# Decoder layer on one core: copies, fill order, last normalisation and PE filler matmuls in attention's last iterations

## The chip, the cores and the metric
The kernel runs on one core of a Trainium2 chip. The metric is the device time of one execution in microseconds (us). A core has five engines that run beside each other and meet at semaphores: PE (TensorE, matrix products and transposes), DVE (VectorE), ACT (ScalarE), POOL (GpSimd) and SP, which here issues DMAs. Each engine takes its instructions in the order in which they were written.

## The reference
The input `x` is 16 blocks of 128 rows by 256 columns. Three sublayers follow each other, each closed by a residual sum and a layer norm over the row.

1. Differential self-attention with 16 heads: `qkv = x @ w_qkv.T`, a rotary turn of q and k, two softmax products whose difference is taken (`sdpa(q1, k1) - lam * sdpa(q2, k2)`), a group norm, and `@ wo.T`.
2. Cross attention over a given context `ctx_512` (16 x 128 x 64): 32 query heads of size 8 share 8 key/value heads; keys and values are both the context.
3. A mixture of experts: a router gives sigmoid scores, the two best of 8 experts are used with normalised weights, and two shared experts see every row. Each expert is `(silu(x @ wg.T) * (x @ wu.T)) @ wd.T`.

Every product must be close to float32. The kernel reaches this by splitting an operand into a float16 high part and a float16 low part (`hi` and `lo`) and adding three products.

## The kernel before
The kernel has two parts: an attention part (both attentions and the router, `build`) and an experts part (`experts`). The second starts when all engines have left the first.

The attention part is a software pipeline over the 16 blocks b. Each engine has a function `body(n)` that is called for n = 0 to 22. In iteration n, stage k works on block n - k where `live(n - k)` holds (0 to 15). Names that begin with `a_` or use `A` belong to self-attention, `c_` or `C` to cross attention. The stages that matter here:

- n - 3, cross attention's stacking. PE transposes the stacked keys (`stack_k`, L905 at the bottom of `stack_T`) and queries (`stack_q`) of the block into one PSUM bank, `c_one`. ACT copies each out of it: `kt_in` (L502, into `c_kt`) and `qm_in` (L494, into `c_qm`). Both use the same bank, so `stack_q` waits for the copy of the keys; and `kt_in` waits until PE has read the previous block's keys for the last time (the eighth `exp_scores` of block n - 4).
- n - 3, at its end, and n - 4. PE fills eight banks of scores (`max_scores`, L937), two of them in iteration n as `max_scores(C, n - 3, 0)` and `1`, six at the beginning of the next. DVE takes the largest of each (`largest`, L680). There are two banks, so fill f waits for the reduction of fill f - 2.
- n - 4. When all eight maxima are there, PE transposes the queries again with their maxima (`restack`, L905), DVE copies them (`reqt_in`, L674), and PE fills eight banks of scores for the exponentials (`exp_scores`, L954), which ACT computes (`exp`, L514), again with two banks. `values_cross` (L982) multiplies the first four with the values (product 0), then the other four (product 1). ACT copies the results out (`ot_in`, L520), and PE turns them back (`back_T`, L992).
- n - 5. DVE divides (`cross_divide`, L749) and scales (`cross_mix`, L756), POOL adds the residual (`cross_add`, L393), DVE takes mean and variance (L706 and L766).
- n - 6. POOL computes the reciprocal root (`power`, L378 and L380) and normalises the block (`normalise`, L385). PE transposes it (`x2_T`, L1023), ACT and DVE split it (`x2_high` L531, `x2_low` L771).
- n - 7. PE computes the router's logits (`route`, L879), DVE copies them out (`logits`, L777).

The order of the work is the order in each engine's `body`. PSUM banks are shared in a fixed cycle (`RINGS` and `Turns`): a PE step waits for the reader of the bank's last content. From n = 16 on self-attention's stages run dry, from n = 19 on cross attention's too. The last blocks then go through with little else beside them.

`keep_warm(k)` (L1037) is k float16 products of 128x128 weights with 240 columns whose result nobody reads. Before the change it is used only for n = 0 to 3, into the bank of `c_one`.

The experts part begins on PE with `group_T(0)` (L1675, eight float32 transposes). ACT and DVE split their result, and PE begins the first expert step (`split_products`, L1684).

Of the kernel before, what the change touches and what calls it, by code (L numbers as in the profile page):

```python
# [15 lines left out]
ALU = mybir.AluOpType  # L16
# [3 lines left out]
P = 128  # L20
B, S, E = 16, 128, 256
# [40 lines left out]
ITERATIONS = B + 7  # L62
WARM = 240
SHARED_HIGH = 3


class Steps:
# [41 lines left out]
def build(nc, a, out):  # L109
    ctx = ExitStack()  # L110
    sems = ExitStack()
    with sems, ctx:
# [116 lines left out]
        def live(b):  # L229

            return 0 <= b < B
# [52 lines left out]
        def _(pool):  # L284
# [110 lines left out]
            def body(n):  # L395

                if live(n - 3):
                    group_norm(n - 3)
                if live(n - 1):
                    q_low(n - 1)  # L400
                if live(n - 4):
                    cross_v(n - 4)
                if live(n - 1):
                    k_low(n - 1)
                if live(n - 6):
                    power(C.mv, C, n - 6, C.s_mv)
                if live(n - 3):
                    cross_k_low(n - 3)
                if live(n - 6):
                    normalise(C.y, C.mv, C, n - 6, x2_ready)  # L410
                if live(n - 5):
                    cross_add(n - 5)
                if live(n - 3):
                    power(A.mv2, A, n - 3, A.s_mv2)
                    normalise(A.y2, A.mv2, A, n - 3, x1_ready)
                if live(n - 2):
                    mix_sub(n - 2)
                if live(n - 3):
                    cross_q_low(n - 3)
                if live(n - 2):  # L420
                    group_scale(n - 2)
                if live(n):
                    rope_sum(n)
# [6 lines left out]
        def _(act):  # L430
# [103 lines left out]
            def body(n):  # L534

                if live(n - 5):
                    ot_in(C, n - 5, 1)
                if live(n - 2):
                    exp(A, n - 2, 0)
                    exp(A, n - 2, 1)  # L540
                if live(n - 1):
                    q_high(n - 1)
                    k_high(n - 1)
                if live(n - 2):
                    exp(A, n - 2, 2)
                    exp(A, n - 2, 3)
                if live(n - 3):
                    y_high(n - 3)
                if live(n - 2):
                    exp(A, n - 2, 4)  # L550
                    exp(A, n - 2, 5)
                    exp(A, n - 2, 6)
                if live(n - 1):
                    kt_in(A, a_one, n - 1)
                if live(n - 2):
                    exp(A, n - 2, 7)
                if live(n - 3):
                    cross_k_high(n - 3)
                if live(n - 2):
                    ot_in(A, n - 2, 0)  # L560
                    ot_in(A, n - 2, 1)
                if live(n - 4):
                    exp(C, n - 4, 0)
                    exp(C, n - 4, 1)
                if live(n - 1):
                    v_in(n - 1)
                if live(n - 4):
                    exp(C, n - 4, 2)
                    exp(C, n - 4, 3)
                if live(n - 6):  # L570
                    x2_high(n - 6)
                if live(n):
                    x_high(n)
                if live(n - 4):
                    exp(C, n - 4, 4)
                    exp(C, n - 4, 5)
                if live(n - 3):
                    cross_q_high(n - 3)
                    kt_in(C, c_one, n - 3)
                if live(n - 4):  # L580
                    exp(C, n - 4, 6)
                    exp(C, n - 4, 7)
                if live(n - 3):
                    qm_in(C, c_one, n - 3)
                if live(n - 4):
                    ot_in(C, n - 4, 0)
                k, half = divmod(n - SHARED_HIGH, 2)
                if 0 <= k < NSH * 3:
                    split_high(act, 0, k, wsh[:, k // 3, k % 3, 0, :], half)
                if live(n - 1):  # L590
                    reqt_in(A, a_one, n - 1)
# [8 lines left out]
        def _(dve):  # L600
# [107 lines left out]
            def moments(t, bn, mv, b, s_bn, s_mv):  # L708

                dve.wait_ge(s_bn, b + 1)  # L710
                dve.memset(t.pad[:], 0.0)
                dve.bn_aggr(mv[:], bn[:]).then_inc(s_mv, 1)
# [47 lines left out]
            def cross_moments(b):  # L760
# [4 lines left out]
                dve.memset(C.pad[:], 0.0)  # L765
                dve.bn_aggr(C.mv[:], C.bn[:]).then_inc(C.s_mv, 1)  # L766

            def x2_low(b):

                dve.wait_ge(A.s_x2hi, b + 1)  # L770
                dve.tensor_tensor(A.x2t_lo[:], c_one[:, 0:E].rearrange("p (c n) -> p c n", c=EC), A.x2t_hi[:],  # L771
                                  ALU.subtract).then_inc(A.s_x2lo, 1)
# [6 lines left out]
            def body(n):  # L779
# [38 lines left out]
                if live(n - 2):  # L818
                    mix_half(n - 2, 1)
                    mix_half(n - 2, 0)  # L820
                if live(n - 6):
                    x2_low(n - 6)
                if live(n - 1):
# [6 lines left out]
                    largest(A, n - 1, 6)  # L830
                if live(n - 2):
                    moments(A, A.bn, A.mv, n - 2, A.s_bn, A.s_mv)
                if live(n - 1):
                    largest(A, n - 1, 7)
                if live(n - 2):
# [10 lines left out]
                    rope_first(n)  # L846
                if live(n - 5):
                    cross_moments(n - 5)
                if live(n):
                    rope_straight(n)  # L850

# [10 lines left out]
        def _(pe):  # L862
# [171 lines left out]

            warm_in = id32[:].bitcast(F16)

            def keep_warm(k):  # L1037

                for _ in range(k):
                    pe.matmul(ps[:, 5, 512 - WARM:], warm_in[:, 0:P], warm_in[:, 0:WARM], start=True, stop=True)  # L1040

            def body(n):

# [49 lines left out]
                    restack(C, c_one, n - 4)  # L1093
                if live(n - 3):
                    out_project(n - 3)
                if n == 1:
                    keep_warm(8)
                if live(n - 1):
# [7 lines left out]
                if live(n - 4):  # L1106
                    exp_scores(C, n - 4, 0)
                    exp_scores(C, n - 4, 1)
                if live(n - 1):
                    max_scores(A, n - 1, 2)  # L1110
                    max_scores(A, n - 1, 3)
                    if n == 1:
                        keep_warm(4)
                    project_v(n - 1)
# [8 lines left out]
                    exp_scores(C, n - 4, 3)  # L1123
                if live(n - 1):
                    max_scores(A, n - 1, 5)
                if live(n - 6):
                    x2_T(n - 6)
                if live(n):
                    x_T(n)
                if n == 0:  # L1130
# [15 lines left out]
                    project_qk(n)  # L1146
                if n == 0:
                    keep_warm(36)
                if live(n - 3):
                    stack_q(C, c_one, n - 3)  # L1150
                if live(n - 2):
                    group_mean(n - 2)
                if 1 <= n < 3:
                    keep_warm(8)
                if live(n - 4):
# [2 lines left out]
                    restack(A, a_one, n - 1)  # L1158
                if 1 <= n < 3:
                    keep_warm(16)  # L1160
                if live(n - 3):
                    max_scores(C, n - 3, 0)
                    max_scores(C, n - 3, 1)
                if live(n - 4):
# [714 lines left out]
```

## Time and profile before

| what | value |
|---|---|
| median of 3 runs | 847.19 us (843.85 to 848.7) |
| profiled execution: device time | 847.25 us |
| profiled execution: span from first to last instruction | 845.0 us |
| mean granted TensorE clock | 0.961 |
| PE busy | 773.2 us (92%) |
| DVE, ACT, POOL busy | 521.2, 519.8, 308.9 us |
| attention part | 0 to 430.1 us of the span |
| experts part | 430.1 to 845.0 us |

Times in the trace are microseconds from the start of the span. "Granted clock" is the share of full speed that the chip gives PE: 1.00 is 2.4 GHz and 0.50 is 1.2 GHz. In a row of a timeline the first number is the start, the second the duration, and what stands in square brackets at its end is how long the engine had been idle before and who ended that.

### The profile page before, as it was taken

To read this page: it belongs to the slowest core of one execution; us is meant where nothing else is said; L and a number is where in the kernel's file an instruction comes from. 1 tells how busy PE (TensorE), PEld (TensorE's weight loads), DVE (VectorE), ACT (ScalarE), POOL (GpSimd) and SP (SyncE) were. 2 spreads that over 40 slices of the span, in tenths; PEclk is the share of its full clock that TensorE was granted. 3 is DMA by queue.
4 is the path that set the end of the run, shared out by engine and by line. 5 is a ranking of instruction groups with operands and counts; after the bars stand their busy time and mean duration, and the time that the engine had idled before them with its cause. 6 is when DMAs were issued, how large, how long until landed. Compare 5 with 4: busy or idle time off the path is not lost.

```text
span 845.0 us, 19993 instructions
## 1 busy us (share of the span) xinstructions
PE 773.2 (92%) x7621; PEld 508.9 (60%) x7621; DVE 521.2 (62%) x1188; ACT 519.8 (62%) x948; POOL 308.9 (37%) x481
## 2 busy tenths in 40 slices
PE   6888999999999999997869899999999999999993
PEld 5555555555555555554435455557878888787652
DVE  3346788888888888865338866764444444444353
ACT  2445788888888888775425554545555655555353
POOL 3134455555555555544210573001222222222222
PEclk9998999999999999998569999999999999999998
DMA  8800000000010100000033676422332322223231
GB/s 247 246 2 1 2 2 33 3 24 11 2 33 2 33 2 2 2 2 1 1 97 97 194 233 201 150 89 51 47 50 45 52 45 49 48 45 52 54 104 63
DMA packets 38282, 51.02 MB, mean 60 GB/s; under 512 B 9264, under 2 KB 33072, under 8 KB 38192
## 3 DMA queue, kind: packets, MB, share of 16 engines
q1 hardware_dynamic: 31040, 40.39, 16.1%
q0 software_dynamic: 7152, 9.34, 6.6%
q8 instruction: 66, 1.08, 0.6%
q14 instruction: 24, 0.20, 0.1%
HBM read 31.04 MB, written 18.68 MB: 59 GB/s over the span
## 4 chain that ended last, share of the span: by engine, by line
PE 39%; DVE 5%; DMA 3%; ACT 2%; issue 1%; POOL 0%; ACTq 0%; POOLq 0%; DVEq 0%
PE ps L1684 34%; PE ps L1763 3%; DMA wst<-in_wx 3%; DVE wr L224 1%; PE ps L1743 1%; DVE ht_lo L1561 1%; DVE th L1556 1%; ACT wr L215 1%; PE ps L1675 0%; ACT th L1402 0%; DVE xg_lo L1549 0%; ACT ht_hi L1407 0%; POOL e_rs L1376 0%; PE ps L1709 0%; ACT xg_hi L1394 0%
## 5 line engine op out<-in xcount | busy, mean ns | idle before, releaser
L1363 POOL DMA_INDIRECT acc<-y_sb,xin x39 | 60.5, 1552 | 220.0 <-ACT y_sb L1431 220.0
L1684 PE MATMUL ps<-wr,xr_hi 128*128 x624 | 129.3, 299 | 0.0
L1402 ACT ACTIVATE th<-ps 128x384 f32<-128x384 f32 (+1 forms) x118 | 57.9, 491 | 108.6 <-PE ps L1684 103.6
L1684 PE MATMUL ps<-xg_hi,wsh 128*128 128x512 f16 x320 | 103.2, 385 | 4.8 <-DVE xg_lo L1549 4.8
L680 DVE TENSOR_REDUCE c_qs<-ps 128x4 f16<-128x512 f32 x128 | 84.0, 693 | 22.6 <-PE ps L937 21.0
L680 DVE TENSOR_REDUCE a_qs<-ps 128x4 f16<-128x512 f32 x128 | 85.1, 689 | 19.7 <-PE ps L937 18.7
L1684 PE MATMUL ps<-wr,xr_lo 128*128 x312 | 93.4, 299 | 0.0
L514 ACT ACTIVATE a_pt<-ps 128x512 f32<-128x512 f32 x128 | 74.5, 595 | 30.4 <-PE ps L954 28.5
L1556 DVE SCALAR_TENSOR_TENSOR th<-th,ps 128x384 f32<-128x384 f32 (+1 forms) x118 | 65.2, 553 | 34.5 <-ACT th L1402 34.4
L514 ACT ACTIVATE c_pt<-ps 128x512 f32<-128x512 f32 x128 | 69.8, 604 | 19.3 <-PE ps L954 19.1
L1643 DVE COPY ht<-ps 128x512 f16<-128x512 f16 x39 | 16.5, 424 | 93.7 <-PE ps L1763 93.7
L1684 PE MATMUL ps<-wr,ht 128*128 x585 | 70.4, 273 | 0.7 <-issue 0.7
L1684 PEld LDWEIGHTS ps<-wr,xr_hi 128*128 128x128 f16 x624 | 59.4, 98 | 18.2
L1684 PEld LDWEIGHTS ps<-wr,ht 128*128 128x128 f16 x585 | 57.0, 98 | 8.0 <-issue 1.3
L1684 PE MATMUL ps<-xg_lo,wsh 128*128 128x512 f16 x160 | 61.6, 385 | 0.0
L1684 PE MATMUL ps<-wsh,ht_hi 128*128 128x256 f16 x320 | 54.7, 273 | 5.4 <-DVE ht_lo L1561 5.2
L1561 DVE TENSOR_TENSOR hs<-th,hs 128x384 f16<-128x384 f32 x78 | 38.3, 492 | 29.1 <-ACT hs L1407 29.1
L1407 ACT ACTIVATE hs<-th 128x384 f16<-128x384 f32 x78 | 36.6, 470 | 31.9 <-DVE th L1556 31.9
L1684 PEld LDWEIGHTS ps<-xg_hi,wsh 128*128 128x128 f16 x320 | 31.7, 99 | 40.6 <-issue 6.8
L948 PE MATMUL ps<-mask,id 128*128 128x512 f16 x128 | 50.2, 392 | 3.2 <-ACT a_qt L508 3.1
L954 PE MATMUL ps<-a_qt,a_kt 32*128 32x128 f16 x512 | 51.0, 219 | 0.0
L954 PEld LDWEIGHTS ps<-a_qt,a_kt 32*128 32x128 f16 x512 | 28.7, 93 | 32.8 <-issue 32.8
(211 smaller groups left out, 1751.1 us busy)
## 6 DMA issues: line engine op xcount, KB each, us to landing
wst<-in_wx SPq DMA_DIRECT2D x30, 640.0 KB, 4.6
xs<-zero SPq DMA_DIRECT2D x1, 5031.0 KB, 19.9
xin<-xs SPq DMA_DIRECT2D x39, 129.0 KB, 2.1
acc<-x_row SPq DMA_DIRECT2D x4, 512.0 KB, 3.3
x_row<-acc SPq DMA_DIRECT2D x8, 256.0 KB, 5.2
out<-x_row SPq DMA_DIRECT2D x8, 256.0 KB, 2.1
x_row<-in_x SPq DMA_DIRECT2D x1, 1536.0 KB, 10.8
wst<-in_wqkvT SPq DMA_DIRECT2D x1, 768.0 KB, 4.8
```

Source lines behind the costliest of these rows:

```text
L514: act.activation(t.pt[:, f, :, :].rearrange("p j n -> p (j n)"), score_bank(t, "e", b, f), ACT.Exp, scale=(E // HEADS if t is A else SD) * ...
L680: dve.tensor_reduce(t.qs[:].rearrange("p (c i) s -> p c i s", i=NI)[:, c:c + 4, f % 4, USED], score_bank(t, "m", b, f).rearrange("p (j n) ...
L948: pe.matmul(o.rearrange("p (j n) -> p j n", j=NI), id16[:], mask4[:].unsqueeze(1).to_broadcast([P, NI, P]), start=True, stop=False, skip_g ...
L954: ins = pe.matmul(o[:, j * P:(j + 1) * P], t.kt[r, c, :], t.qt[r, c, :], start=t is C, stop=True, skip_group_check=t is A)
L1363: pool.indirect_dma_start(acc, bass.IndirectOffsetOnAxis(ap=row, axis=0), y_sb[:, n % 2, :], None, compute_op=ALU.add).then_inc(f_acc, 16)
L1402: act.activation(th[:, k % 2, 0:n], gate[:, k % 2, 0:n], ACT.Silu, scale=1.0 / WSCALE).then_inc(f_th, 1)
L1407: act.activation(dst, th[:, k % 2, 0:dst.shape[-1]], ACT.Copy).then_inc(f_hhi, 1)
L1556: dve.scalar_tensor_tensor(out=t, in0=t, scalar=1.0 / WSCALE, in1=up[:, k % 2, 0:n], op0=ALU.mult, op1=ALU.mult).then_inc(f_hid, 1)
L1561: dve.tensor_tensor(dst, th[:, k % 2, 0:dst.shape[-1]], hi, ALU.subtract).then_inc(f_hlo, 1)
L1643: dve.tensor_copy(ht[:, HALVES[1][0]:, :, :].rearrange("p j r n -> p (j r n)"), htp[1]).then_inc(f_hTin[1], 1)
L1684: ins = pe.matmul(o, l[x], r[y], start=(first and n == 0), stop=(last and n == m - 1), skip_group_check=not (first and last))
L1763: ins = pe.transpose(htp[half][:, o:o + P], hs[:, r, j * P:(j + 1) * P], id16[:])
```

## The change
`LAST = B + 1` is 17, the first iteration without a block of self-attention in stage n - 1. The edits act from n = 17 on.

- The two copies `kt_in` and `qm_in` of cross attention go from ACT to DVE for n = 17 and 18 (blocks 14 and 15). On DVE `kt_in` stands behind `x2_low(n - 6)`, ahead of the moments of block n - 5, and `qm_in` behind these.
- For n = 17 and 18 PE's `max_scores(C, n - 3, 0)` and `1` stand ahead of `values_cross(n - 4, 1)`, no longer behind it.
- `normalise` of block 15 goes from POOL to DVE (`last_normalise`), in n = 21.
- `keep_warm` gets a bank as argument and is called in n = 17 to 21 with `a_one`, a bank that no stage uses by then: 8 products ahead of `stack_q` (n = 17, 18); 6 behind the place of `out_project` and 4 behind the second `exp_scores` (n = 18, 19); 10 ahead of product 1 (n = 19); 8 ahead of `x2_T` (n = 20, 21) and 5 behind it (n = 19, 20, 21). By iteration, n = 17 to 21, that is 8, 18, 25, 13 and 13 products.

```diff
@@ POOL body
-                if live(n - 6):
+                if live(n - 6) and n - 6 < B - 1:
                     normalise(C.y, C.mv, C, n - 6, x2_ready)
@@ ACT body
                     cross_q_high(n - 3)
-                    kt_in(C, c_one, n - 3)
+                    if n < LAST:
+                        kt_in(C, c_one, n - 3)
...
-                if live(n - 3):
+                if live(n - 3) and n < LAST:
                     qm_in(C, c_one, n - 3)
@@ DVE
+            def last_normalise():
+
+                dve.wait_ge(C.s_rstd_ok, B)
+                dve.tensor_scalar(x_all[:, B - 1, :], C.y[:], C.mv[:, 0:1], C.rstd[:, 0:1], ALU.subtract, ALU.mult
+                                  ).then_inc(x2_ready, 1)
@@ DVE body
+                if n - 6 == B - 1:
+                    last_normalise()
                 if live(n - 6):
                     x2_low(n - 6)
...
                     moments(A, A.bn, A.mv, n - 2, A.s_bn, A.s_mv)
+                if live(n - 3) and n >= LAST:
+                    kt_in(C, c_one, n - 3)
...
                 if live(n - 5):
                     cross_moments(n - 5)
+                if live(n - 3) and n >= LAST:
+                    qm_in(C, c_one, n - 3)
@@ PE
-            def keep_warm(k):
+            def keep_warm(k, bank=c_one):
 
                 for _ in range(k):
-                    pe.matmul(ps[:, 5, 512 - WARM:], warm_in[:, 0:P], warm_in[:, 0:WARM], start=True, stop=True)
+                    pe.matmul(bank[:, 512 - WARM:], warm_in[:, 0:P], warm_in[:, 0:WARM], start=True, stop=True)
@@ PE body
                     out_project(n - 3)
+                if n in (LAST + 1, LAST + 2):
+                    keep_warm(6, a_one)
...
                     exp_scores(C, n - 4, 1)
+                if n in (LAST + 1, LAST + 2):
+                    keep_warm(4, a_one)
...
+                if n in (LAST + 3, LAST + 4):
+                    keep_warm(8, a_one)
                 if live(n - 6):
                     x2_T(n - 6)
+                if n in (LAST + 2, LAST + 3, LAST + 4):
+                    keep_warm(5, a_one)
...
+                if n in (LAST, LAST + 1):
+                    keep_warm(8, a_one)
                 if live(n - 3):
                     stack_q(C, c_one, n - 3)
+                if n == LAST + 2:
+                    keep_warm(10, a_one)
                 if live(n - 2):
                     group_mean(n - 2)
+                if n >= LAST and live(n - 3):
+                    max_scores(C, n - 3, 0)
+                    max_scores(C, n - 3, 1)
...
                 if live(n - 4):
                     values_cross(n - 4, 1)
...
-                if live(n - 3):
+                if live(n - 3) and n < LAST:
                     max_scores(C, n - 3, 0)
                     max_scores(C, n - 3, 1)
```

## Rows read from the trace of the kernel before

**Rows 1.** The page's 40 slices of 21.1 us: granted TensorE clock in tenths.
```profile
PEclk9998999999999999998569999999999999999998
```

**Rows 2.** Busy time by stage of the drain; columns: stretch, length, busy us (instructions) per engine, clock, DMA.
```profile
366.70:386.04 19.34, 17.56 (x214) 9.98 (x211) 11.43 (x32) 15.50 (x29) 8.54 (x17) 1.00 0.00 1
386.13:404.56 18.43, 15.19 (x129) 8.19 (x130) 8.81 (x22) 9.06 (x18) 7.87 (x17) 0.72 0.00 1
404.56:422.98 18.42, 14.98 (x111) 8.29 (x112) 7.68 (x18) 6.09 (x12) 4.55 (x7) 0.58 0.00 1
422.98:430.10 7.12, 1.73 (x17) 0.81 (x15) 2.48 (x10) 0.77 (x2) 2.61 (x5) 0.50 0.00 0
430.10:439.33 9.23, 7.69 (x24) 3.71 (x25) 1.53 (x3) 3.28 (x5) 0.32 (x2) 0.55 0.65 192
```

**Rows 3.** The same view, in stretches between changes of the granted clock.
```profile
387.14:390.56 3.42, 2.70 (x32) 1.65 (x30) 3.34 (x7) 0.99 (x3) 1.73 (x6) 1.00 0.00 0
390.56:393.97 3.41, 3.16 (x20) 2.07 (x21) 2.49 (x7) 0.00 (x0) 2.51 (x3) 0.50 0.02 5
393.97:397.38 3.41, 2.64 (x31) 1.46 (x34) 1.55 (x6) 3.00 (x7) 1.95 (x3) 1.00 0.00 0
...
400.80:404.21 3.41, 2.92 (x20) 1.09 (x22) 0.00 (x0) 2.84 (x5) 0.00 (x0) 0.50 0.00 0
404.21:407.62 3.41, 2.69 (x34) 1.67 (x32) 3.06 (x6) 0.60 (x1) 2.16 (x4) 1.00 0.02 5
```

**Rows 4.** Groups by line, 366.6 to 430.1 us: busy, mean ns, idle before.
```profile
L680 DVE TENSOR_REDUCE c_qs<-ps 128x4 f16<-128x512 f32 x24 | 15.2, 690 | 11.2 <-PE ps L937 10.9
L514 ACT ACTIVATE c_pt<-ps 128x512 f32<-128x512 f32 x24 | 13.0, 600 | 13.3 <-PE ps L954 13.3
...
L385 POOL TENSOR_SCALAR x_row<-c_y,c_mv,c_rstd 128x256 f32<-128x256 f32 x5 | 6.1, 1225 | 0.3
...
L674 DVE COPY c_qt<-ps 128x1024 f16<-128x1024 f16 x3 | 2.1, 691 | 1.3 <-PE ps L905 1.2
...
L502 ACT ACTIVATE c_kt<-ps 128x1024 f16<-128x1024 f16 x2 | 2.0, 1023 | 2.5 <-PE ps L954 2.5
```

**Rows 5.** PE's timeline, 383 to 428 us.
```profile
383.58 0.61 PE L905 MATMUL ps<-id,c_qs 128*128 128x128 f16 x8 [1.31 <-ACT c_kt L502]
...
384.71 1.07 PE L982 MATMUL ps<-c_pt,c_v 128*32 128x512 f32 x8 [0.34 <-DVE a_g L730]
...
393.95 0.41 PE L954 MATMUL ps<-c_qt,c_kt 32*128 32x128 f16 x8
...
401.29 1.01 PE L905 MATMUL ps<-id,c_qs 128*128 128x128 f16 x8 [1.31 <-ACT c_kt L502]
402.24 1.93 PE L982 MATMUL ps<-c_pt,c_v 128*32 128x512 f32 x8
...
411.66 0.61 PE L954 MATMUL ps<-c_qt,c_kt 32*128 32x128 f16 x8 [0.79 <-DVE c_qt L674]
...
418.90 1.94 PE L982 MATMUL ps<-c_pt,c_v 128*32 128x512 f32 x8 [1.16 <-ACT c_pt L514]
...
422.77 0.63 PE L1023 MATMUL ps<-id,x_row 128*128 128x128 f32 x2
...
427.58 0.69 PE L1023 MATMUL ps<-id,x_row 128*128 128x128 f32 x2 [2.85 <-POOL x_row L385]
```

**Rows 6.** DVE's timeline, 423 to 425 us.
```profile
423.86 0.42 DVE L771 TENSOR_TENSOR a_x2t_lo<-ps,a_x2t_hi 128x256 f16<-128x256 f32 x1
424.65 0.43 DVE L706 BATCH_NORM_STATS2 c_bn<-c_y 128x6 f32<-128x256 f32 x1 [0.37 <-POOL c_y L393]
```

**Rows 7.** PE's timeline at the kernel's beginning: `keep_warm`.
```profile
3.59 5.11 PE L1040 MATMUL ps<-id 128*128 128x240 f16 x26
...
28.38 1.80 PE L1040 MATMUL ps<-id 128*128 128x240 f16 x16
```

**Rows 8.** The chain that ended last, behind the attention part: start, us, what.
```profile
433.58 5.10 PE ps L1684 x12
```

More of the change, by code:

```diff
@@ L64 @@
 SHARED_HIGH = 3
+LAST = B + 1
 class Steps:
```

## Prediction
> **What bounds the kernel now.** I read the page's slices first. The granted clock is near full except at the kernel's edges and in three slices about 380 to 443 us [rows 1], where attention runs dry. The stage table comes next: the last full iteration of the drain has clock 1.00, the two after it 0.72 and 0.58, the tail of the last block 0.50, the entry into the experts 0.55 [rows 2]. No engine is saturated there: in 404.56 to 422.98 PE is busy 14.98 of 18.42 us, DVE 7.68, ACT 6.09, and each works while the others wait. It is one block's chain: eight reductions on DVE, a transpose and a copy, eight exponentials on ACT, two value products, two transposes and copies for the next block, then again. The bounds of the stages are the starts of DVE's reductions of blocks 14 and 15, 386.13 and 404.56; 422.98 is the end of block 15's last transpose back. So each iteration's length is the chain's length, and PE's speed enters it wherever PE is the one awaited: the stack transposes take 0.61 at full clock and 1.01 at half, the value product 1.07 and 1.93 [rows 5].
>
> What the clock does: in 387.14 to 390.56 PE only hands small score fills to DVE (busy 2.70 of 3.42, though), and the clock falls to half at its end. In 390.56 to 393.97 it has transposes and the output projection with hardly a gap, and the clock returns. In 393.97 to 397.38 it waits for ACT between fills (2.64), and it falls. In 400.80 to 404.21 a stack and a value product stand back to back, and it returns. In the fills for DVE after that (2.69) it falls again [rows 3] and stays at half to the end of attention and 8 us beyond: 0.58, 0.50, 0.55 [rows 2].
>
> The Trainium skill (TensorE: Matmul & The Clock Gate, "Why this matters for your kernels") asks for no long idle gaps between bursts. By that rule alone the clock would not have fallen here, because PE is busy four fifths of each of those stretches; the trace disagrees. By the rule the filler products would change no clock and be pure cost, which is rival C below; by the rows they stand where gaps preceded a fall.
>
> **The change part by part.** The sum is made against the profiled execution, 847.25 us, which lies at the median, 847.19.
>
> *Price of a filler product.* 16 took 1.80 at full clock, so 0.10 each after a tail of about 0.2; 26 took 5.11 near the start, 0.19 to 0.20 each, which is twice that and so the price at half [rows 7].
>
> *n = 17 (clock 1.00).* The key copy goes from 1.02 on ACT to 0.69, the price of DVE's copy of the same shape [rows 4], and the query copy likewise: 0.33 each. The 8 fillers (0.8) lie in the 1.31 us in which PE awaits the key copy [rows 5], 0.95 after the change, so they cost 0. DVE then starts block 14's reductions about 0.7 early. But value product 1 (0.85 of issue) and a transpose back (0.45) now stand behind the first two score fills and ahead of the third, for which DVE waits after two reductions (1.3 us). Before, the product lay under the query copy. So nearly all is given back: 0.15 gained (bounds 0 and 0.7).
>
> *n = 18.* The reductions (15.2 busy for 24, so 0.64 each [rows 4]) are as before, and so is the fall of the clock. Behind the output projection PE went straight into the exponentials' fills at 393.95, with no idle time [rows 5]: 6 fillers there are on the chain, 0.6 at full clock and 1.2 at half; the clock returned at 393.97, so 0.5 lost (bounds 0.4 and 1.2). The 4 fillers behind the second fill lie in a wait for ACT, at 0. They fill the stretch whose gaps came before the fall, so I take full clock up to the next reductions. What that gives, each term a half-clock duration less a full-clock one: product 0 about 0.5, key stack 0.4, two fills 0.2, query stack 1.01 - 0.61 = 0.4 [rows 5]; the two copies 0.33 each [rows 4]; product 1, which ended at 404.17, some 0.8 behind the query copy (401.29 + 1.01 + 1.03 = 403.4), leaves the chain, 0.75. Together 2.9, less 0.5, against 0.3 of finer overlaps: DVE starts 2.7 early. Product 1 and the transpose ahead of the third fill take 0.5 back. Gained 2.2 (bounds 0.3, if the clock stays at half and 8 fillers of 1.6 outlast the wait, and 3.2).
>
> *n = 19.* The reductions let the clock fall again. At half, the transposed queries and 6 fillers (1.2) end 0.3 behind DVE's copy, so the first fill is 0.3 late. The fillers, the transposes and the fills stand close together, as in 390.56 to 393.97, so I expect the return 1 to 2 us into the exponentials; 4 fillers partly at half cost 0.4 to 0.5 once. At full clock this leg is ACT's: 24 exponentials are 13.0 busy, 0.54 each [rows 4]; 0.43 to the first, four (2.2), `x2_high` 0.4, two (1.1), 0.4 behind product 0, two (1.1): product 1 begins 5.6 behind the first fill. It was 418.90 - 411.66 = 7.24 [rows 5], so 1.65. The 10 fillers (1.0) lie in the wait for the last exponential, 1.16 before. Product 1 gives 1.94 - 1.07 = 0.87. Its end to 422.98 was 2.14 and becomes about 1.35 (copy 0.6, four transposes at full clock 0.6): 0.8. Sum 3.3, less 0.8: 2.5 (bounds -2.6, worked out under C, and 3.5).
>
> *n = 20 and 21.* The 8 fillers ahead of block 14's `x2_T` push it back by 0.8. DVE's `x2_low(14)` stands ahead of the statistics of block 15, and started 0.79 before them [rows 6]; behind the fillers it ends some 0.3 after POOL's sum is ready: 0.3 lost (1.5 at half clock). The last normalisation was 1.22 on POOL [rows 4]. DVE has no such row, so bounds: 0.17, a tiny operation, and 0.69; I take 0.42, that of the 128x256 operations [rows 6]. 0.8 gained. The last `x2_T` at full clock: 0.2. The other fillers lie under POOL's power and under ACT's and DVE's split. Sum 0.7.
>
> The Trainium skill (VectorE: DVE Perf Modes, the errata section's cycle table) gives an SBUF-source operation 58 cycles plus elements over the mode's factor at 0.96 GHz, an estimate of 0.2 us for this one; by it the sum would gain another 0.2. No row here shows this operation in SBUF.
>
> *Entry into the experts.* The mean clock of 0.55 over 430.10 to 439.33 [rows 2] says that half clock held until about 438.3. Eight transposes and 12 products (5.10) are on the chain there [rows 8], 7 us of PE at half; all at full clock would save 3.4. But PE waits about 1.5 between them for the split (9.23 less 7.69 busy) and has little before; I expect the clock to hold for a part, 1.4 (bounds 0 and 3.4). DVE's routing work follows PE's first result, so this passes on.
>
> Sum: 0.15 + 2.2 + 2.5 + 0.7 + 1.4 = 7.0. 847.25 - 7.0 = **840.2 us**.
>
> **The rivals.** B, the clock comes back in one of the two long iterations only, or returns late in each: where the changes of clock fall against the work decides that, and the runs of before differ by 4.9 us among themselves. That loses some 2 of the drain's 5.6 and the entry's 1.4: gain 3.5, **843.7**.
>
> C, the fillers pay for nothing (slower): the clock doesn't return, and they cost 0.2 each wherever PE is awaited. n = 18: 1.2 ahead of the fills, 0.3 beyond the wait ahead of the query stack, less 0.33 and 0.7 of copy and reorder, +0.5. n = 19: 0.3, 0.4, 1.0 (5 ahead of fill 4) and 0.9 (10 at 2.0 in 1.16), +2.6. n = 20: +1.5. Normalisation -0.8. Sum +3.8: **851.0**. It decides once n = 19's fillers run at half. For it: PE was already busy four fifths and lost its clock. Against: each return followed dense work, and fillers are the densest there is.
>
> D, the clock also holds through reductions and entry: 2 more at the entry, 1 at n = 19: **837**.
>
> E, the drain gains its 5.6, but the entry gives nothing, since PE waits there with the clock gone or the constants' loads come last: **841.7**.
>
> F, the change doesn't do what it says: the score fills put ahead gain DVE nothing, as the third comes no earlier. That is in my sum; were it absent, DVE's earlier start would stay, 1.0 more.
>
> **How the numbers follow.** Chances: forecast 0.52 (own range 838 to 843), B 0.22, C 0.09, D 0.07, E 0.10. The range takes D at its low end and B with 3 us of scatter at the high end: 836.5 to 847. Within 0.5% (843.0 to 851.4), about what a measurement can tell from no change, lie three fifths of B, half of C and a little of the forecast: 0.22. Slower, the other half of C and accidents: 0.06. Faster: 0.72.
>
> **What would show it.** Right: granted clock above 0.85 in n = 18 behind the exponentials' start and above 0.8 in n = 19; product 1 of blocks 14 and 15 near 1.07; DVE's reductions of block 15 some 2.7 early, but a gap of about 0.7 behind the second; block 15's chain from its last maximum to its last transpose back 10.7 long, not 13.3; `last_normalise` near 0.42. Wrong: a clock of 0.50 with L1040 at 0.2 each in n = 19; the third fill with no wait; or an experts part longer than the 415 us of before.

## The result, and the profile after

The changed kernel takes 838.87 us (median of 4 runs, 837.29 to 842.1), the kernel before 847.58 (4 runs, 843.85 to 848.7): ratio 0.9915, 95% interval 0.9887 to 0.9944. Run again beside other kernels (e10 below, 5 runs) it took 838.94, ratio 0.9884 (0.9848 to 0.992). The forecast was 840.2. Its total was right. One of its terms was not, and in the profiled execution 2.3 us from outside the changed part made up for it, which is luck.

Line numbers have moved: `max_scores` is L951, `exp_scores` L968, `values_cross` L996, the stack transposes L919, `back_T` L1006, `x2_T` L1037, `keep_warm` L1054, `largest` L682, DVE's copies L671, L664 and L676.

The page's clock line answers to [rows 1]: of the three low slices none below 0.8 is left.

```profile
PEclk9997999999999999999899999999999999999997
```

The stages of the drain, cut at the same events as [rows 2] (first reduction of block 14, of block 15, end of the last transpose back, `group_T`, end of the first silu); columns as there:

```profile
384.81:403.54 18.73, 16.00 (x150) 9.48 (x154) 10.28 (x25) 7.10 (x15) 7.88 (x16) 0.82 0.00 1
403.54:419.92 16.38, 14.87 (x145) 9.08 (x146) 7.79 (x18) 6.30 (x12) 4.86 (x8) 0.90 0.01 2
419.92:426.05 6.13, 3.92 (x42) 2.97 (x40) 2.88 (x11) 0.77 (x2) 1.39 (x4) 1.00 0.00 0
426.05:433.70 7.65, 6.11 (x24) 2.83 (x25) 1.55 (x4) 3.27 (x5) 0.32 (x2) 0.78 0.56 158
```

The second line is 16.38 us long where it was 18.42, the third 6.13 for 7.12. But the first is 18.73 for 18.43: although its clock rose from 0.72 to 0.82, the iteration did not get shorter. The same view in stretches of one clock, against [rows 3]:

```profile
390.98:394.39 3.41, 3.26 (x20) 2.44 (x20) 2.31 (x7) 0.00 (x0) 1.50 (x2) 0.50 0.02 5
394.39:397.80 3.41, 3.15 (x36) 1.78 (x38) 0.57 (x3) 2.86 (x7) 1.98 (x3) 1.00 0.00 0
397.80:401.22 3.42, 3.42 (x28) 1.60 (x21) 0.44 (x2) 1.60 (x5) 0.64 (x1) 0.50 0.00 0
...
408.04:411.46 3.42, 3.42 (x22) 2.58 (x22) 2.81 (x7) 0.00 (x0) 0.73 (x1) 0.50 0.00 0
411.46:428.52 17.06, 13.09 (x135) 8.69 (x133) 4.92 (x19) 8.09 (x17) 3.68 (x8) 1.00 0.03 6
428.52:431.94 3.42, 3.28 (x8) 1.19 (x9) 0.59 (x1) 1.05 (x1) 0.00 (x0) 0.50 0.61 177
```

In n = 18 the clock fell behind 397.80, as it had behind 397.38 before, although the 4 fillers stood ahead and PE was busy for 3.15 of the 3.41 us that led up to it (2.64 before). In n = 19 it came back at 411.46 and stayed to 428.52, through the rest of attention and into the experts; before, it was at half from 407.62 to 438.3. PE's timeline has the steps that [rows 5] has (same columns):

```profile
384.71 1.07 PE L996 MATMUL ps<-c_pt,c_v 128*32 128x512 f32 x8
385.71 0.66 PE L1006 MATMUL ps<-id,c_ot 128*128 128x128 f32 x4
386.30 0.41 PE L951 MATMUL ps<-c_kt,c_qm 24*128 24x128 f16 x8
...
393.22 1.35 PE L1054 MATMUL ps<-id 128*128 128x240 f16 x6
394.51 0.41 PE L968 MATMUL ps<-c_qt,c_kt 32*128 32x128 f16 x8
...
417.41 1.07 PE L996 MATMUL ps<-c_pt,c_v 128*32 128x512 f32 x8
```

The third score fill starts at 386.30, behind the value product and the transpose; that is the reorder's price. The 6 fillers at 393.22 stand between the output projection and the first exponential fill for their full 1.35. Product 1 of block 15 takes 1.07, no longer 1.94. DVE's timeline shows the wait behind the second reduction, and the last normalisation:

```profile
384.81 1.29 DVE L682 TENSOR_REDUCE c_qs<-ps 128x4 f16<-128x512 f32 x2 [0.49 <-PE ps L951]
386.73 2.49 DVE L682 TENSOR_REDUCE c_qs<-ps 128x4 f16<-128x512 f32 x4 [0.63 <-PE ps L951]
...
423.33 0.41 DVE L773 TENSOR_SCALAR x_row<-c_y,c_mv,c_rstd 128x256 f32<-128x256 f32 x1 [0.86 <-POOL c_rstd L381]
```

### The profile page after: what moved, and what is told of

The parts are those of the page before. It is cut to its first block and busy times, and to the rows that moved or that the text cites. A ratio compares the mean times of both kernels' runs of the same rounds, so it can differ in the third digit from the quotient of the medians.

```text
span 837.6 us, 20147 instructions
## 1 busy us (share of the span) xinstructions
PE 774.1 (92%) x7698; PEld 512.9 (61%) x7698; DVE 524.6 (63%) x1193; ACT 516.2 (62%) x944; POOL 309.3 (37%) x480
## 5 line engine op out<-in xcount | busy, mean ns | idle before, releaser
L682 DVE TENSOR_REDUCE a_qs<-ps 128x4 f16<-128x512 f32 x128 | 85.2, 690 | 18.8 <-PE ps L951 17.9
L682 DVE TENSOR_REDUCE c_qs<-ps 128x4 f16<-128x512 f32 x128 | 84.4, 694 | 16.7 <-PE ps L951 15.3
L515 ACT ACTIVATE c_pt<-ps 128x512 f32<-128x512 f32 x128 | 69.7, 603 | 21.1 <-PE ps L968 20.8
L968 PE MATMUL ps<-a_qt,a_kt 32*128 32x128 f16 x512 | 51.8, 222 | 0.0
L968 PEld LDWEIGHTS ps<-a_qt,a_kt 32*128 32x128 f16 x512 | 29.2, 94 | 33.5 <-issue 33.5
```

The lines of the kernel that those rows point to most:

```text
L515: act.activation(t.pt[:, f, :, :].rearrange("p j n -> p (j n)"), score_bank(t, "e", b, f), ACT.Exp, scale=(E // HEADS if t is A else SD) * ...
L682: dve.tensor_reduce(t.qs[:].rearrange("p (c i) s -> p c i s", i=NI)[:, c:c + 4, f % 4, USED], score_bank(t, "m", b, f).rearrange("p (j n) ...
L968: ins = pe.matmul(o[:, j * P:(j + 1) * P], t.kt[r, c, :], t.qt[r, c, :], start=t is C, stop=True, skip_group_check=t is A)
```

## The experiments

The whole difference between two kernels is a few us, and one execution differs from the next by as much. So each kernel's trace was cut at the same events, and the steps are compared as well as the times. t0 is the end of block 13's last exponential fill; "3rd" is the start of the third reduction, "last" the end of the eighth, "fill" the start of the first exponential fill, "back" the end of block 15's last transpose back. One execution each, us:

```
step                  before  changed    e1     e2     e3     e4     e5     e6     e7     e8     e9    e10
t0 to 3rd, b14          5.06     5.09   6.84   5.06   4.74   5.08   5.08   5.46   5.08   4.75   4.75   5.07
3rd to last, b14        4.18     4.19   4.64   4.18   4.18   4.19   5.01   4.20   4.19   5.00   4.59   4.19
last to fill, b14       2.43     3.59   2.48   3.19   3.45   2.47   2.37   3.46   3.39   1.75   1.75   3.33
fill b14 to 1st, b15   10.61     9.03  10.48   8.55   9.26  10.86   7.74   9.83   9.18   7.88   7.89   9.24
1st to 3rd, b15         1.20     1.92   3.46   1.21   1.21   1.93   1.92   1.92   1.92   1.21   1.21   1.92
3rd to last, b15        3.88     3.88   4.08   3.67   3.67   3.69   4.38   3.68   3.89   4.36   4.07   3.88
last to fill, b15       2.02     2.27   2.01   2.36   2.36   2.36   1.61   1.61   2.36   1.61   2.43   2.36
fill to product 1       7.24     5.80   7.26   8.33   5.93   8.35   5.80   5.80   7.88   8.54   5.80   7.83
product 1 to back       4.08     2.51   4.07   2.51   2.51   2.50   2.50   2.50   2.51   2.50   2.51   2.50
back to last route      6.40     5.42   5.53   6.29   5.42   5.42   5.42   5.42   5.42   5.27   5.27   5.43
t0 to group_T          47.86    44.45  51.60  46.10  43.48  47.59  42.58  44.63  46.76  43.81  41.20  46.50
group_T to 1st silu     8.56     6.96   8.76   7.85   7.05   5.36   6.99   6.93   5.36   5.35   5.36   7.80
1st silu to end       406.25   404.52 405.40 407.81 404.87 405.40 404.55 404.81 406.35 405.86 409.84 405.35
```

("Last route" is the start of the fourth of its six products.) Each column is one execution, and some were not typical of their kernel: e1's was the third slowest of 12 (850.23 us, clock 0.948 for a mean of 0.958), e4's the slowest of 12 (845.33, clock 0.967 for 0.973), e10's the slowest of 5.

**e1: everything but the fillers.**

```diff
-                if n in (LAST + 1, LAST + 2):
-                    keep_warm(6, a_one)
...
-                if n == LAST + 2:
-                    keep_warm(10, a_one)
```

> The changed kernel without its 77 filler products; copies, reorder and last normalisation stay. Theory (the clock is what gains): the granted clock stays at about 0.58 in iteration n = 19, product 1 of block 15 takes 1.93, the entry into the experts (start of group_T to the first silu) takes 8.6 us as before, and the kernel gains only 0.33 x 2 from the copies in n = 18, up to 0.7 from the reorder, and 0.8 from the normalisation: 1.5 to 2.3 us, ratio 0.9975. Rival (the engine moves carry it): 5 us or more, ratio 0.994 or lower, at an unchanged clock.

Measured: 845.97 (12 runs, 841.38 to 852.07), ratio 0.9995 (0.9966 to 1.0024). The engine moves alone give nothing that can be measured. The medians are 0.6 apart where 1.5 to 2.3 were expected, and the interval takes in both. In its trace, one of its slow executions, the clock fell once and stayed at half for 58 us:

```profile
384.54:442.56 58.02, 44.67 (x291) 23.14 (x292) 23.24 (x57) 17.18 (x33) 15.19 (x31) 0.50 0.09 27
```

The normalisation's gain is there all the same: back to last route 5.53 for 6.40. At half clock the reorder is worse than at full: the wait behind the second reduction is 2.17, for 0.63 in the changed kernel.

```profile
385.71 1.29 DVE L682 TENSOR_REDUCE c_qs<-ps 128x4 f16<-128x512 f32 x2 [0.70 <-PE ps L951]
389.18 2.69 DVE L682 TENSOR_REDUCE c_qs<-ps 128x4 f16<-128x512 f32 x4 [2.17 <-PE ps L951]
```

**e2: the fillers alone.** Copies, order and normalisation as before.

```diff
-                if n >= LAST and live(n - 3):
-                    max_scores(C, n - 3, 0)
-                    max_scores(C, n - 3, 1)
...
-                if n - 6 == B - 1:
-                    last_normalise()
```

> The kernel before with the 77 filler products alone; both copies on ACT, the fill order and the last normalisation as before. Theory: full clock in n = 19 and at the entry, so 2.5 + 1.6 us less the waits that the fillers add (1.2 in n = 18, 0.2 in n = 20): 3 to 5 us, ratio 0.995. Rival: no gain or a loss, since the fillers run at half clock, 0.2 us each, wherever PE is awaited: ratio 1.000 to 1.005.

Measured: 844.88 (12 runs, 837.11 to 849.11), ratio 0.9981 (0.9953 to 1.001), which falls between what the two expected. In this trace n = 18 ran at full clock (8.55 from fill to reductions) and n = 19 at half (8.33 from fill to product 1).

Neither half does what both together do. Each run also reports its mean granted clock, and that shows why:

```
kernel            runs   mean us   mean clock   us for 0.01 of clock (fit over its runs)
before              61     847.3        0.958   6.1
e1 no fillers       12     846.6        0.958   4.2
e2 fillers alone    12     844.9        0.969   6.5
changed              4     839.3        0.977   4.9
changed, e10         5     839.4        0.975   5.3
```

By the means the moves alone give 0.7 us, the fillers alone 2.4, both at once 8.0; the intervals of e1 and e2 lie clear of that of the changed kernel. The fillers alone raise the clock by 0.011, the moves alone not at all, both by 0.017 to 0.019. The time follows the clock within each kernel, with 0.8 to 1.6 us of scatter about the line. The fillers have a cost of their own: at a mean clock of 0.966, where both have runs, the lines of the kernel before and of e2, which differ by the fillers alone, stand at 842.5 and 847.0 (an estimate, read off the fits). That the moves let the fillers work, because the gaps they leave are shorter, fits all this. It is argued and not shown: no run traces it step by step, and e2's one trace held full clock in n = 18, where the changed kernel lost it.

**e3: the reorder undone.**

```diff
-                if n >= LAST and live(n - 3):
-                    max_scores(C, n - 3, 0)
-                    max_scores(C, n - 3, 1)
...
-                if live(n - 3) and n < LAST:
+                if live(n - 3):
```

> The changed kernel with the first two score fills behind value product 1 again, as before. Theory (the reorder gives back what it gains, for the product and the transpose stand ahead of the third fill): in n = 17 at full clock DVE's reductions of block 14 start within 0.3 us of where they start with the reorder, counted from the last exponential fill, there is no gap behind the second, and the third ends 0 to 0.7 us earlier; time within 0.3% of the changed kernel's. Rival (the reorder helps): the third reduction comes 0.5 to 1.0 us later in both iterations, and the kernel takes 1 to 2 us more.

Measured: 839.42 (10 runs), ratio 0.9917 (0.9886 to 0.9949), the changed kernel's own. In the steps: block 14's reductions start 0.38 later than with the reorder, and the third starts 0.35 earlier (4.74 for 5.09); from block 14's fill to block 15's third reduction 10.47 for 10.95. In these two traces the reorder costs 0.3 to 0.5 in each iteration; in the times it can't be seen.

**e4: without the 6 fillers of n = 18.**

```diff
-                if n in (LAST + 1, LAST + 2):
+                if n == LAST + 2:
                     keep_warm(6, a_one)
```

> The changed kernel without the 6 fillers behind the output projection in n = 18 (those in n = 19 stay). Theory (they stand on the chain, at half clock): the first exponential fill of block 14 starts 1.2 us earlier, counted from the last reduction, and the whole is 0.6 to 1.3 us faster than the changed kernel. Rival (they bring the clock back, or hold it): without them the stretch behind the output projection runs at half clock for longer, the reductions of block 15 start no earlier, and the time is the same or 1 us longer.

Measured: 841.73 (12 runs, 835.18 to 845.33), ratio 0.9923 (0.9895 to 0.9951), mean clock 0.973. The fill came 1.12 earlier (2.47 for 3.59), as the theory said, but in this trace the clock did not return behind it, and fill to reductions took 10.86 for 9.03, as the rival said. That the missing fillers kept it down is not shown: the kernel before has no fillers there either, and its clock returned at 393.97 [rows 3]. The median is 2.9 above the changed kernel's, on the rival's side, but the intervals overlap.

```profile
392.30:405.96 13.66, 13.37 (x93) 8.07 (x92) 6.00 (x18) 6.40 (x14) 5.14 (x7) 0.50 0.01 1
```

**e5: fillers between the score fills too.**

```diff
                     max_scores(C, n - 4, 2)
+                if n in (LAST + 1, LAST + 2):
+                    keep_warm(3, a_one)
...
                     max_scores(C, n - 4, 7)
+                if n in (LAST + 1, LAST + 2):
+                    keep_warm(3, a_one)
```

> The changed kernel with 3 more fillers behind each of the score fills 2 to 5 and 7 in n = 18 and 19, that is while DVE reduces (30 more products). Theory (the clock is lost in the reductions and its return costs the stretch behind them): no fall to half clock between the reductions of block 14 and group_T in any of the two iterations, transposed queries 0.61 and the 6 fillers 0.6 instead of 1.2, from the last reduction of block 14 to the first of block 15 about 10.8 instead of 12.6 us, mean clock over the span 0.985 or more, 2 to 4 us faster than the changed kernel. Rival (fillers in the reductions delay the score fills for which DVE waits): third to last reduction longer than 4.2 us, no gain.

Measured: 838.5 (6 runs, 835.18 to 846.82), ratio 0.99 (0.9857 to 0.9943). Both were half right. The clock never fell in the drain:

```profile
384.77:401.82 17.05, 15.07 (x165) 9.35 (x169) 10.57 (x24) 7.10 (x15) 7.85 (x16) 1.00 0.00 1
401.82:418.03 16.21, 15.39 (x160) 9.45 (x161) 8.00 (x18) 6.30 (x12) 4.84 (x8) 1.00 0.01 2
```

Fill to reductions fell from 9.03 to 7.74, last reduction to fill from 3.59 to 2.37 with the 6 fillers still in. But 3 fillers are more than PE's wait between two score fills holds: block 14's reductions took 5.01 for 4.19, block 15's 4.38 for 3.88. Net 1.9 less from t0 to `group_T`. Of the 2 to 4 us that the theory expected, the medians show 0.4, within the noise, and the mean clock was 0.981, not 0.985.

**e6: the copies on ACT again.**

```diff
-                    if n < LAST:
-                        kt_in(C, c_one, n - 3)
+                    kt_in(C, c_one, n - 3)
```

> The changed kernel with both copies of cross attention on ACT again. In runs so far the fillers alone gained 1.6 us and the engine moves alone 0.4, but both 7 to 8. Theory (each wait that the copies shorten is also one that costs clock, so the copies matter with fillers): about half of the way back to the fillers-only kernel, 842 to 843 us, with a mean clock of about 0.973. Rival (the copies are worth their 0.33 us each and no more): 0.7 to 1.4 us slower than the changed kernel, 840 us, mean clock 0.977.

Measured: 842.16 (12 runs), ratio 0.9937 (0.9907 to 0.9967), mean clock 0.974. The median lies where the theory had it, but its interval overlaps the changed kernel's. The steps give the copies' plain worth: t0 to the third reduction 5.46 for 5.09, and from fill to third reduction of block 15 11.75 for 10.95; 1.2 in two iterations.

**e7: fillers at the entry into the experts.**

```diff
             for n in range(ITERATIONS):
                 body(n)
+            keep_warm(4, a_one)
...
             group_T(0)
+            warm_in = id32[:].bitcast(F16)
+            for _ in range(12):
+                pe.matmul(ps[:, 3, 512 - WARM:], warm_in[:, 0:P], warm_in[:, 0:WARM], start=True, stop=True)
```

> The changed kernel with 4 fillers behind the last route and 12 behind group_T(0), in the 1.5 us in which PE awaits the split. Theory (PE at half clock was on the chain at the entry): group_T to the first silu 5.4 to 5.7 us instead of 7.0, 1.3 to 1.6 us faster. Rival (the entry's time is hidden behind the weights' loads for DVE's and ACT's splits): the same entry, but the time from the first silu to the end is longer by as much, no gain.

Measured: 840.98 (6 runs), ratio 0.9899 (0.9864 to 0.9934). The entry took 5.36, as expected, and it passes on: from the first split of group 0 to that of group 1 43.58 for 44.98 (46.50 in the kernel before). In the whole it can't be seen: in this trace n = 19 ran at half clock (7.88 for 5.80), and from the first silu to the end it took 1.8 more than the changed kernel's (406.35 for 404.52), as the rival said. But 1.3 of these lie behind the first transpose of the routed experts (280.87 for 279.55 to the end), where the clock was at half from 561.27 to 564.68, and not in waits for weights.

**e8, e9, e12: all of it.** e8 is e3 with the fillers of e5 and e7, without the 6, and with the 8 fillers of n = 20 behind `x2_T`. e9 has 2 fillers behind each score fill, not 3, and keeps the 6 in n = 19. e12 is e9 again. Parts of e9's edit against the changed kernel:

```diff
                     max_scores(C, n - 4, 2)
+                if n in (LAST + 1, LAST + 2):
+                    keep_warm(2, a_one)
...
-                if n in (LAST + 1, LAST + 2):
+                if n == LAST + 2:
                     keep_warm(6, a_one)
...
-                if n in (LAST + 3, LAST + 4):
+                if n == LAST + 4:
                     keep_warm(8, a_one)
...
-                    keep_warm(5, a_one)
+                    keep_warm(13 if n == LAST + 3 else 5, a_one)
```

> Fillers in the reductions and at the entry as in the two kernels above, no reorder, no 6 fillers behind the output projection, and in n = 20 the 8 fillers behind x2_T instead of ahead of it. Theory: full clock from the first reduction of block 14 on, the first exponential fill of block 14 within 2.4 us of the last reduction, that of block 15 within 1.8, t0 to group_T 40 us instead of 44.5, entry 5.5; 832 to 834 us, mean clock 0.99. Rival: the clock still falls somewhere in the drain, and the time is that of the changed kernel, 839, within 1.5 us.

> As the combined kernel, but 2 instead of 3 fillers behind each score fill, and the 6 fillers stay in n = 19, where PE awaits DVE's copy, though not in n = 18. Theory (3 fillers were more than the wait between two score fills holds, and the 6 in n = 19 hold the clock for block 15's exponentials): third to last reduction of block 14 within 4.4 us instead of 5.0, half clock nowhere between the reductions of block 14 and the experts, t0 to group_T about 40 us, the whole 832 to 835 us, 4 to 6 faster than the changed kernel. Rival (the experts part gives it back in its waits for weights): t0 to the first silu shorter by 6 but the whole within 2 us of the changed kernel's.

> e9 again. Its trace was 4.8 us ahead of the changed kernel's at the experts' first silu and 0.6 at the end. Theory (what was given back lay in the first two groups, by a stretch at half clock and loads of weights that landed late in that execution): in this trace at least half of the lead is left at the end, and the median is 836 to 838 us. Rival (the experts part runs to a time set by the loads, whatever comes before it): again from the first silu to the first routed transpose 127 us or more, and 838 to 840 us.

Measured: e8 839.07 (6 runs), ratio 0.989 (0.9854 to 0.9925); e9 838.81 (6), 0.9883 (0.985 to 0.9917); e12 837.64 (6), 0.9884 (0.9853 to 0.9915). e8 missed its theory and met its rival: the clock fell at 409.62, fill to product 1 took 8.54, and t0 to `group_T` 43.81, not 40. e9's steps came near: the reductions took 4.59 (4.4 expected, 5.00 in e8), and 41.20 + 5.36 = 46.6 from t0 to the first silu, for 51.4 in the changed kernel and 56.4 before, although the clock fell once more, from 403.55 to 406.97. The whole didn't follow, as its rival said: from the first silu to the end e9's trace took 409.84 for 404.52. Of these 5.3, 3.6 lie in the second group of experts and 1.7 behind the first routed transpose (281.22 for 279.55), where the clock was at half from 557.15 to 560.57. From first split to first split group 0 took 43.4 to 43.6 in e7, e9 and e12, but group 1 took 45.88 in e9, 44.82 in e12, 44.48 in e11 below and 43.56 in e8, for 42.31 in the changed kernel, 41.72 in e10 and 42.62 in e7. The first four had a stretch at half clock at group 1's head, the others none; e12's:

```profile
467.57:470.99 3.42, 3.42 (x10) 1.28 (x9) 1.98 (x3) 0.00 (x0) 2.83 (x4) 0.50 0.67 214
```

and in e9 one load of weights on the chain took 7.62, where the changed kernel has 4.6 to 5.3:

```profile
492.37 7.62 DMA wst<-in_wx
```

Why the clock falls there in these kernels is open. e12's trace met part of both expectations: of its lead of 6.6 at the first silu 4.4 was left at the end, and its median is 837.6, as the theory had it, but from the first silu to the first routed transpose it took 127.5, the rival's sign. Against the changed kernel's 9 runs (mean 839.3) the 12 of e9 and e12 have a mean of 837.8: by the intervals not a difference that these runs establish.

**e10: the changed kernel again.**

> The changed kernel again, on the chip and beside the runs of the one above. Theory (when the clock changes falls differently in each execution): the same 839 us median within 1.5, a spread of 5 us or more over the runs that follows the mean granted clock of each, about 5 us for 0.01; the trace shows other stretches at half clock than the first did, with steps between them of the same length at the same clock. Rival (the time is settled by the program alone): the same stretches at half clock to 0.1 us, counted from t0.

Measured: 838.94 (5 runs, 836.93 to 843.71). The profiled execution took 4.0 us more than the first one did, with the same instructions. Its steps up to the fill of block 15 agree within 0.3 us; then the clock stayed at half to 418.03, where it had returned at 411.46:

```profile
407.79:418.03 10.24, 10.13 (x69) 5.72 (x66) 4.30 (x12) 3.53 (x7) 2.10 (x4) 0.50 0.00 0
```

and fill to product 1 took 7.83 for 5.80, entry 7.80 for 6.96. That is rival B of the prediction, as a property of an execution and not of the kernel.

**e11: fillers at the switch to the routed experts too.**

```diff
+            pe.wait_ge(f_hid, HR - 1)
+            for _ in range(12):
+                pe.matmul(ps[:, 0, 512 - WARM:], warm_in[:, 0:P], warm_in[:, 0:WARM], start=True, stop=True)
             pe.wait_ge(f_glo, EC * NG)
             x_T(0)
             w = weights_of(0)
+            for _ in range(4):
+                pe.matmul(ps[:, 0, 512 - WARM:], warm_in[:, 0:P], warm_in[:, 0:WARM], start=True, stop=True)
```

> e9 with 16 more fillers at the switch from shared to routed experts: 12 in the 1.5 us in which PE awaits the last split, 4 behind the first transpose of a routed tile. Theory (in the kernels that enter this point with the clock at an edge, half clock for some 3.4 us behind it costs 1.5: from the first such transpose to the end 280.7 to 281.2 us in four traces with it, 278.9 to 279.6 in eight without): 279.5 here, no half clock between 550 and 600 us. Rival (the fillers delay the first tile's work): 280 or more at full clock.

Measured: 837.79 (6 runs, 834.73 to 840.66), ratio 0.9884 (0.985 to 0.9917). From the first routed transpose to the end 279.27 us, with no half clock behind the switch, as the theory had it. But e12, without these fillers, had none either and took 279.25; so the fillers cost nothing that can be seen, and their use isn't shown.

## Why the prediction was right, and where it was not

Point by point, on the two first traces (span 845.0 and 837.6, so 7.4; forecast 7.0):

- **n = 17**: forecast 0.15, measured 0.0. The reductions started 0.70 earlier (forecast 0.7), and the third start came at 5.09 from t0 for 5.06. The give-back by the product and the transpose is as described, and complete.
- **n = 18**: forecast 2.2, measured -0.3 (third reduction of block 14 to third of block 15: 18.73 for 18.43). This is the step that failed. It said of the 4 fillers "They fill the stretch whose gaps came before the fall, so I take full clock up to the next reductions". The clock fell behind 397.80 all the same. Product 0 and the key stack kept their half-clock durations, and the 6 fillers ran at half, their upper bound, 1.2 for the 0.5 taken. In steps: 1.6 was gained from fill to reductions (9.03 for 10.61), 1.15 was lost at the 6 fillers (3.59 for 2.43) and 0.7 behind the second reduction of block 15. So of its signs two failed: the clock behind the exponentials' start was 0.81, not above 0.85, and block 15's reductions came 0.4 early from t0, not 2.7. It was no accident of one execution: in e3, e6, e7 and e10 too the clock fell in this place. Why it fell with PE busy for 3.15 of 3.41 us stays open. e5 shows that the size was there to be had at full clock: 7.74 + 2.37 from last reduction to first, for 12.62 in the changed kernel and 13.04 before. The low bound of 0.3 was itself too high.
- **n = 19**: forecast 2.5, measured 2.8 (third reduction to transpose back 14.45 for 17.21). Product 1 began 5.80 behind the first fill, forecast 5.6; the first fill was 0.25 late, forecast 0.3. The clock came back at 411.46, just ahead of the first fill at 411.61 and not 1 to 2 us behind it, so the 4 fillers did not cost the 0.4 to 0.5 set down for them. From block 15's last maximum to its last transpose back it took 10.57, forecast 10.7. In e10, where the clock returned later, this term was 2.1 smaller.
- **n = 20 and 21**: forecast 0.7, measured 1.0. The normalisation took 0.41, forecast 0.42; the fillers ahead of `x2_T` cost 0.15, forecast 0.3, by 5.42 against 5.27 in e8 and e9. The Trainium skill (VectorE: DVE Perf Modes, the errata section's cycle table) gave an estimate of 0.2 for the normalisation; the trace's 0.41 decides against it.
- **Entry**: forecast 1.4, measured 1.6 (6.96 for 8.56). e7 shows that 1.6 more was there; together that is 3.2, near the upper bound of 3.4.
- **The rest**: forecast 0, measured 1.7 behind the first silu and 0.6 ahead of t0, where the kernels do the same. The 1.7 includes group 1, 42.31 for 43.68, with loads of weights on its chain of 5.28 and 4.89 for 5.98 and 5.53. Nothing of the change acts there, and in e10, the same program, the two together are 1.2, not 2.3; I count it as luck.

So the miss of 2.5 in n = 18 was covered by 2.3 from outside the changed part: in this trace the changed part gave 5.0 us of the forecast 7.0. Over many runs the size is right all the same, 839.3 on average over 9 runs against 847.3, or 8.0; which steps gave it in the runs that were not traced isn't known. Rival B, at 3.5, is what e10's trace shows: 2.1 from t0 to the first silu and 1.2 elsewhere. Rival C (fillers pay for nothing) has its conditions met in one iteration at a time, never in all; e2 comes closest, at 0.9981 and not slower. Rival F, in the sum, was right: e3's third reduction comes earlier without the reorder.

## What to carry to other kernels

Where short steps of several engines wait for each other in turn, the TensorE clock is a term of the sum, and filler products can be worth more than the moves between engines that they stand beside; here neither was worth much without the other, and why is argued only. Put fillers where PE waits in any case and no more of them than the wait holds; a filler ahead of a step on the chain is paid in full, and twice over at half clock (6 took 1.35 us here). And where the clock's changes move from one execution to the next, compare kernels by steps of equal clock and by many runs: the same program's two traces differed here by 4.0 us.

## What the runs showed of the hardware that was not expected

- The clock could stay at half for 58.02 us (e1) in a stretch in which PE counts as busy for 44.67, and for 13.66 us (e4) in one with 13.37 busy. PE's longest idle gap in the first was 1.98 us, in the second 0.18. The Trainium skill (TensorE: Matmul & The Clock Gate, "Why this matters for your kernels") asks for a TensorE that is kept busy, and for no long idle gaps between bursts. By that the clock should have returned in the second stretch, and the trace disagrees. What brings it back is open.
- The mean granted clock, in the records of each run, accounts for most of the spread between runs of one kernel: 4.2 to 6.8 us for 0.01 in the kernels with ten runs or more, whose runs spread over 10 to 13 us.
- A half-clock stretch of 3.4 us just behind the switch to the routed experts cost 1.5 us (278.9 to 279.8 without, 280.7 to 281.2 with), near the half of its length.
